# Layer 1's lists, expert weights and gate/up products, and layer 0's row gathers, in a two-layer mixture-of-experts kernel

## The reference

```
x = x + tanh(g_xattn[0]) * L0_xattn(layernorm(x), ctx, ...)   # router picks 2 of 64 context rows a token
x = x + tanh(g_ffn[0])   * L0_ffn(layernorm(x), ...)          # 32 experts, 6 a token, at most 192 tokens an expert
x = x + tanh(g_xattn[1]) * L1_xattn(layernorm(x), ctx, ctx)   # 16 heads, causal mask, 64 context rows
x = x + tanh(g_ffn[1])   * L1_ffn(layernorm(x), ...)          # 8 experts, 2 a token, and a shared expert

# an expert of L1_ffn: inner size I = 352
out = silu(x @ gw) * (x @ uw) @ dw
acc = acc + combine_weight[:, None] * out
```

## Time and profile before

| | |
|---|---|
| timed runs | 1188.62, 1192.48, 1199.31 us; median 1192.48 |
| the profiled execution | 1201.21 us, its span 1199.4 us |
| stage 1, until about | 235 us |
| stage 2 | 235 to 570 us |
| stage 3, and the wait for weights behind it | 570 to 868 us |
| stage 4 | 868 to 1199 us |
| busy share over the span | PE 89%, DVE 40%, POOL 32%, ACT 28% |

### The profile page before, as it was taken

The page is one execution under the profiler, slowest core; times in us unless marked ns, Lnnn a source line. Parts: engine busy times, 40 slices in busy tenths (PEclk is TensorE's granted clock), DMA queues, the critical chain, the costliest instruction groups (busy, mean ns, idle before and its releaser), DMA issues.

```text
span 1199.4 us, 13046 instructions
## 1 busy us (share of the span) xinstructions
PE 1063.8 (89%) x4351; PEld 707.0 (59%) x4351; DVE 480.3 (40%) x1148; ACT 331.4 (28%) x529; POOL 384.2 (32%) x340
## 2 busy tenths in 40 slices
PE   5777969579979999999599999899799999999995
PEld 4333424168769888886276766656355566556553
DVE  5767687224324444432684756451111111111110
ACT  3444441023323443332223423211012221222221
POOL 0003767625444555553002002220023233233322
PEclk9867979879989999999899999999899999999998
DMA  9110111379989989984503104219822332333330
GB/s 329 77 53 23 32 36 45 97 266 258 249 267 277 248 240 249 245 198 59 194 18 41 66 9 45 36 37 293 364 37 55 71 62 51 66 68 57 58 71 8
DMA packets 52801, 148.52 MB, mean 124 GB/s; under 512 B 12244, under 2 KB 12628, under 8 KB 47297
## 3 DMA queue, kind: packets, MB, share of 16 engines
q1 hardware_dynamic: 24752, 81.09, 21.4%
q0 software_dynamic: 24160, 44.03, 19.2%
q10 hardware_dynamic: 3824, 22.57, 5.5%
HBM read 109.76 MB, written 41.08 MB: 126 GB/s over the span
## 4 chain that ended last, share of the span: by engine, by line
PE 64%; DMA 15%; DVE 8%; issue 4%; POOL 4%; ACT 3%; SPq 0%; ACTq 0%; POOLq 0%; DVEq 0%
PE pb L586 16%; PE pb L602 8%; DMA acc_rows<-big 7%; PE pb L456 6%; PE pb L559 6%; PE pb L315 5%; PE pb L317 5%; PE pb L316 5%; DMA big<-hn_rows,big 4%; PE pb L322 4%; PE pb L378 3%; DVE big L908 2%; POOL list_rows L1300 2%; DVE big L916 2%; POOL acc_rows L1331 2%
## 5 line engine op out<-in xcount | busy, mean ns | idle before, releaser
L586 PE MATMUL pb<-big 128*128 x624 | 193.7, 464 | 5.5 <-issue 5.5
L456 PE MATMUL pb<-big 128*128 128x192 f32 x1024 | 174.9, 330 | 2.1 <-ACT bigr L746 1.3
L456 PEld LDWEIGHTS pb<-big 128*128 128x128 f32 x1024 | 170.9, 193 | 6.1 <-issue 2.8
L586 PEld LDWEIGHTS pb<-big 128*128 128x128 f32 x624 | 116.7, 192 | 65.0 <-issue 8.0
L1331 POOL DMA_INDIRECT acc_rows<-big x64 | 95.9, 1498 | 138.8 <-DMA acc_rows<-big 47.8
L1300 POOL DMA_INDIRECT list_rows<-big x96 | 93.9, 978 | 139.0 <-DVE big L920 110.4
L315 PE MATMUL pb<-bigr 128*128 128x512 f32 (+2 forms) x320 | 132.2, 413 | 4.4 <-DVE bigr L908 3.5
L1358 POOL DMA_INDIRECT out<-big x39 | 61.8, 1585 | 207.3 <-ACT big L888 207.3
L316 PE MATMUL pb<-bigr 128*128 128x512 f32 (+2 forms) x320 | 127.5, 399 | 0.0
L317 PE MATMUL pb<-bigr 128*128 128x512 f32 (+2 forms) x320 | 127.3, 398 | 0.0
L916 DVE SCALAR_TENSOR_TENSOR big<-pb,big 128x512 f32<-128x512 f32 (+1 forms) x80 | 58.8, 735 | 143.4 <-PE pb L559 41.4
(11 more groups left out here) (124 smaller groups left out, 1160.7 us busy)
## 6 DMA issues: line engine op xcount, KB each, us to landing
big<-in_we SPq DMA_DIRECT2D x32, 1024.0 KB, 7.9
rawr<-in_we SPq DMA_DIRECT2D x32, 512.0 KB, 4.3
big<-in_we ACTq DMA_DIRECT2D x1, 8704.0 KB, 37.0
hn_rows<-big SPq DMA_DIRECT2D x32, 256.0 KB, 2.0
big<-in_we ACTq DMA_DIRECT2D x1, 6528.0 KB, 34.1
big<-in_x SPq DMA_DIRECT2D x4, 1024.0 KB, 15.4
acc_rows<-big SPq DMA_DIRECT2D x16, 256.0 KB, 4.7
big<-acc_rows SPq DMA_DIRECT2D x16, 256.0 KB, 4.3
```

Of the source, the lines that this page charges most:

```text
L456: r = e.matmul(ps[:, m * CAP:(m + 1) * CAP], WR[b % 4][:, at_:at_ + 128], XT[b % 2][:, k, :], start=(k == 0), stop=(k == 3))
L586: r = e.matmul(ps[:, 0:I1], XT1[b % 2][:, k, :], W1[:, bass.ds(r0 + (q * 4 + k) * I1, I1)], start=(k == 0), stop=(k == 3))
```

## The change

1. **Layer 1's lists on TensorE.** `scatter1`, `lists1` and `turnl1` go. For each half block, DVE builds one-hot matrices of the list slots (`hote`, `hotv`, 128x512 each), POOL multiplies one of them by the token number and by the rounded weight (`hot`, two 128x512 products), PE multiplies them (`hotm`, four fp32r matmuls of 384 columns), DVE sums (`lsum`, 128x384). At the end come `lsumw`, `lturn`, `lcopy`, `lsel` and `ids1`.
2. **Experts loaded one by one.** `w1a` and `w1b` on ACT's queue become eight steps `w1.0` to `w1.7` on SP's queue, each with a semaphore of its own; `w1.0` waits for `hotm.3.1`, `w1.4` for the last shared gate product. Tile b below 8 waits only for expert b. The copies of tiles 0 and 1 also wait until all of `put3` have landed (`l_o`), since their memory is reused.
3. **Three rounded gate and up products.** `upt` becomes `gatet` and `upt`, each 12 fp32r matmuls of 352 columns. For each tile ACT rounds the expert's gate and up weights (`wgh`, `wuh`: 128x1408 each) and DVE takes the rest (`wgl`, `wul`), and the transposed rows are split in the same way (`turnt` on ACT and now on DVE). Register reads of ETK stand on ACT, DVE and PE.
4. **Layer 0's rows three experts ahead.** Six buffers G in place of four; `fetch.n+3` stands where `fetch.n+2` stood; `fetch.2` also waits for the stores of `acc_rows`.
5. The tables `PE_1`, `ACT_1`, `DVE_1` and all of stage 3's are in a new order.

Its core:

```diff
+                    three(e, PB[2 + 2 * (b % 2) + q][:, 0:I1], [(XH1[b % 2][:, k, :], XL1[b % 2][:, k, :], wh[:, k * I1:(k + 1) * I1], wl[:, k * I1:(k + 1) * I1])
+                                                               for k in range(4)]).then_inc(s_pe, c.up())
...
+                elif kind in ("wgh", "wuh"):
+
+                    q, user = dict(wgh=(0, "gatet"), wuh=(1, "upt"))[kind]
+                    if b < E1:
+                        e.wait_ge(l_w1[b], 16)
+                    if b < 2:
+                        e.wait_ge(s_dve, dve_end3)
+                        e.wait_ge(s_pe, pe_end3)
+                        e.wait_ge(l_o[0], 128)
+                        e.wait_ge(l_o[1], 128)
+                    else:
+                        e.wait_ge(s_pe, pe(user, b - 2))
+                    if q == 0:
+                        regs[b] = e.value_load(ETK[0:1, b:b + 1], min_val=0, max_val=7 * WE1)
+                    prev()
+                    e.activation(WSP[b % 2][q][0], w1[:, bass.ds(regs[b] + 4 * I1 * q, 4 * I1)], ACT.Copy).then_inc(s_act, c.up())
...
+                    tensor(lo, w1[:, bass.ds(regs[b] + 4 * I1 * q, 4 * I1)], hi.bitcast(F32), ALU.subtract)
...
+                elif kind == "w1":
+
+                    if b == 0:
+                        e.wait_ge(s_pe, pe("routet1", 3))
+                        e.wait_ge(s_pe, pe("flip3", 3, 3))
+                        e.wait_ge(s_pe, pe("hotm", 3, 1))
...
+                    e.dma_start(S(b * WE1, WE1, mem=w1), a["we1"][b]).then_inc(l_w1[b], 16)
...
-        pool2 = words(lambda n: (f"fetch.{n + 2} " if n + 2 < E0 else "") + (f"add.{n - 1}" if n else ""), E0) + f" add.{E0 - 1}"
+        pool2 = "fetch.2 " + words(lambda n: (f"fetch.{n + 3} " if n + 3 < E0 else "") + (f"add.{n - 1}" if n else ""), E0) + f" add.{E0 - 1}"
```

More of the change, by code:

```diff
@@ L47, in constants @@
     c[:, C_INV:C_INV + 128] = 1.0 / 64
-    c[:, C_TK1:C_TK1 + 16] = p[:, None] + 128 * np.array(TILES)
+    c[:, C_TK1:C_TK1 + 16] = p[:, None] + 128 * np.array(TILES) + 1
+    c[:, C_TP] = 2049 + p
     l0 = np.zeros((TRASH0, 2), np.float32)
     l0[:, 0] = 2048 + np.arange(TRASH0) % CAP
[L51 to L57, removed]
@@ L59 @@
[L59 removed]
+    return c, l0
@@ L118, in program @@
         rawr = second_name("rawr", 17152, 34816, F32)
+        hots = second_name("hots", 1536, 3600, F32R)
+        BACK = REST_ + NCONST + 4 * D + 4 + 4 + 64 + 64
+        later = second_name("later", BACK, 53120, F32R)
+        slots = second_name("slots", BACK, BACK + 32 * I1, F32R)
+        inner = second_name("inner", BACK + 32 * I1 + 2048, 53120, F32)
+        with nc.sbuf_tensor("w1", [128, REST_], F32) as w1:
+            pass
         big = ctx.enter_context(nc.sbuf_tensor("big", [128, 53120], F32))
@@ L212, in program @@
         YS = [two(D, p1=HALF) for _ in range(4)]
+        G[4], G[5] = two(D, p1=HALF), two(D, p1=HALF)
         LB = ring(HALF, 2, p1=64)
@@ L572, in _ @@
                     else:
[L573 removed]
+                        e.wait_ge(s_dve, dv("turnt", b - 1))
                     flip(e, G1[b % 2], PB[0]).then_inc(s_pe, c.up())
[L575 to L580 removed]
+                elif kind in ("gatet", "upt"):
+                    q = 0 if kind == "gatet" else 1
+                    wh, wl = WSP[b % 2][q]
+                    e.wait_ge(s_dve, dv("turnt", b))
+                    e.wait_ge(s_dve, dv("wgl" if q == 0 else "wul", b))
                     if b >= 2:
                         e.wait_ge(s_dve, dv("mult", b - 2))
[L583 to L587 removed]
+                    three(e, PB[2 + 2 * (b % 2) + q][:, 0:I1], [(XH1[b % 2][:, k, :], XL1[b % 2][:, k, :], wh[:, k * I1:(k + 1) * I1], wl[:, k * I1:(k + 1) * I1])
+                                                               for k in range(4)]).then_inc(s_pe, c.up())
                 elif kind == "flipt":
@@ L893, in _ @@
             c = Counter()
+            regs = {}
             def prev():
@@ L1274, in _ @@
                     both(AC1[j % 2], PB[j][:, :], TG[:, 3:4], xr[b][:, j, :], ALU.mult, ALU.add)
+                elif kind == "turnt":
+                    e.wait_ge(s_act, av("turnt", b))
+                    if b >= 2:
+                        e.wait_ge(s_pe, pe("upt", b - 2))
+                    tensor(XL1[b % 2].rearrange("p a b -> p (a b)"), PB[0][:, :], XH1[b % 2].rearrange("p a b -> p (a b)").bitcast(F32), ALU.subtract)
+                elif kind in ("wgl", "wul"):
+                    q, user = dict(wgl=(0, "gatet"), wul=(1, "upt"))[kind]
+                    hi, lo = WSP[b % 2][q]
+                    e.wait_ge(s_act, av(kind[0:2] + "h", b))
+                    if b < E1:
+                        e.wait_ge(l_w1[b], 16)
+                    if b >= 2:
+                        e.wait_ge(s_pe, pe(user, b - 2))
+                    if q == 0:
+                        regs[b] = e.value_load(ETK[0:1, b:b + 1], min_val=0, max_val=7 * WE1)
+                    tensor(lo, w1[:, bass.ds(regs[b] + 4 * I1 * q, 4 * I1)], hi.bitcast(F32), ALU.subtract)
                 elif kind == "mult":
```

284 lines of the change are left out of this document (174 added, 110 removed).

## The result

The changed kernel is slower: 1227.86 us median of four runs (1218.82 to 1237.64) against 1191.99, a ratio of 1.028 (1.021 to 1.035). In a second measurement (e14) it was 1.031 (1.024 to 1.037). I had predicted 1192.0 and no change, with 1214.0 as the upper end of the range.

A forecast was written before the change was run, and what follows sets the result against it. Bounds: POOL's list writes ending stage 1, a chain of adds in stage 2, PE in stages 3 and 4, the weight load between. Terms +4 − 5 + 5.5 + 1 + 14 + 2 − 22 = −0.5 gave 1192.0 us, range 1172 to 1214.

The forecast's parts named there:

- Stage 2: Layer 0's experts: gathering rows three ahead gains only for the first six experts, −5 us (−12 to 0).
- the chain of adds stays: Stage 2: POOL's adds in HBM stay 9.53 us apart, though PE's 22.4 us of waits could go.
- my rivals: Stores not held, 1179.5 (0.12); stage 4 at PE's pace, 1179 (0.13); longer circle, 1214 (0.15); late lists, 1204 (0.10).
- the upper bound of 0: Stage 2: the slow end of the range −12 to 0 us for gathering rows three experts ahead.
- The transition: Between stages 3 and 4: stores land behind loads, first `gatet` 52.6 us after `w1.0`'s issue, +14 us (+9 to +19).
- rival one: Between stages 3 and 4: stores are not held behind loads, 12.5 us less, 1179.5 us; chance 0.12.
- Stage 4: Gate and up in fp32r: a circle through the engines gives 7.51 us a tile against 8.08, saving 22 us.
- The lists: Stage 3: `hotm` adds 5.5 us on PE, the other list and order terms net +1 (−4 to +10).
- the 1.8 that hide them: Stage 3: POOL's products stay hidden while each takes less than 1.8 us; +2 us put on them.
- the 1 us that I had named as a sign: Stage 3: the changed profile should show `hotm` without waits of over 1 us.
- Stage 1: End of stage 1: the new order ends `place.3` some 11 us later, 6.7 hidden, +4 us (0 to +8).
- The sum: Whole kernel: all terms together come to −0.5 us, 1192.0 us predicted; chance 0.50.

The follow-up runs named there:

- e14: The changed kernel unedited, measured again beside other runs on one chip: 1238.31 us, 1.031 of the kernel before.
- e3: The kernel before with only layer 0's rows gathered three experts ahead (six buffers): 1224.62 us, 1.019 of before.
- e1: The changed kernel with layer 0's rows gathered two experts ahead again (four buffers, old POOL order): 1210.43 us, 1.010 of before.
- e2: The changed kernel with `split` ahead of `yout` on ACT and DVE in stage 2: 1209.72 us, 1.004 of before.
- e10: The changed kernel with the 1 MB load ahead of the 0.5 MB load on SP's queue in stage 2: 1213.75 us, 1.017 of before.
- e11: The changed kernel with six output buffers in place of four in stage 2: 1206.91 us, 1.010 of before.
- e4: The changed kernel with the last stores between the weight loads on SP's queue: 1211.25 us, 1.007 of before.
- e7: The changed kernel with loads `w1.0` to `w1.7` on ACT's queue and the stores alone on SP's: 1218.7 us, 1.024 of before.
- e13: The changed kernel with `split` ahead of `yout`, `turnt` ahead of `wuh`, and the expert loads on ACT's queue: 1181.06 us, 0.985 of before.

## Why the prediction was wrong

**Stage 2 is the step that failed.** I wrote that with rows three experts ahead PE's waits could go, "but the chain of adds stays", and put −5 on it with 0 as the upper bound. Three things were wrong in that. PE's waits for rows did not go: they are 28.6 us in stage 2, 22.4 before. The chain of adds has no pace of its own: the adds are 6.7 to 7.5 us apart at the end of stage 2, behind the last weight load (landed at 550.7), and 7.0 to 13.7 ahead of that, by what is under way beside them. And I did not ask what PE, when it runs further ahead of the adds, reaches next: the output buffers, two experts deep, with `yout` at the head of DVE's queue. Before, `yout` hardly had to wait (4.6 us for adds in all of stage 2 on DVE, against 119.3 after). The change added that wait on DVE, where `split` and behind it 1.5 MB of loads stand in line. This is the question that I had put to SP's queue at the transition, and did not put to DVE's in stage 2. None of my rivals had it; the upper bound of 0 had no reason behind it that excluded a loss. That the cause is this line of waits is shown by e3, which adds the fetch alone to the kernel before, and by e1, e2, e10 and e11, which each take away another link of it: with all links the adds take 310.7 to 312.6 in six traces and 318.3 in a seventh, with one of them missing 273.5 to 295.8 in eleven.

**The transition** was right in kind: stores behind loads in one queue, shown by e4, and rival one, shown by e7 to hold only for two queues. The size was 57.7 in place of 52.6 from issue to first gate product. `put3.3.0` landed 48.6 behind `w1.0`'s issue where I had 45.3, and the two stores and copies took 9.1 in place of 7.3. In rival one I had misread a row and left out a price: 861.46 is `out3.3.3`, not `out3.3.2`, and for a landing beside loads I had 3, where three of before's own last stores took 10.3, 12.9 and 12.4 us. With such landings the first `gatet` comes after 44 us, as in e7, and not after 40.

**Stage 4** was right to 0.13 us a tile: 7.64 against 7.51, the term that was short being the gaps at ACT (0.18 ahead of `wuh`) and PE's 0.20 behind DVE. Copies took 1.38 and 1.63, against 1.40 and 1.63. Passes of 352 columns followed at 0.16. Over 39 tiles the 0.13 are 5 us. The first two tiles took 9.5 and 9.2, some 3 more together than two of the rest, for which I had 2: PE had waited for 25 us ahead of tile 0, its granted clock fell from 1.00 to 0.50 (the lower of its two levels, 1.2 GHz) in that wait, and the first passes, up to 923.6, follow at 0.29. By the Trainium skill, TensorE: Matmul & The Clock Gate, The mechanism (Part 3), a weight load overlaps matmuls in flight only where its row group differs, so the 24 loads should have stood between the passes; the trace disagrees here too, for 24 passes from 999.75 take 3.9 us with a load in each. The same section names loads into a background weight buffer as a second case; which buffer these loads went to no run shows.

**The lists** cost 8.9 for 6.5 (7.7 as the mean of all traces with the lists, against the two without). POOL's products took 1.24 on average, under the 1.8 that hide them, one of the sixteen 1.94, and `hotm` waited for DVE's `hotv` for 2.4 in all, about the 2 that I had put on POOL; one of these waits was 1.40, over the 1 us that I had named as a sign. PE's long wait at the front of the stage is 12.4 in place of 8.8, where I had 3 more, and the wait of 4.08 is gone, as I had it. The rest, `hote`, `hotv` and `lsum` on DVE, I had not costed as waits of others, and no run tells it apart.

**Stage 1**: a wait of POOL of 5.03 where I had 4. Its effect on the time was not shown by the undo, and over all traces the first add comes 1.6 later with the new tables, so most of the +6.4 in the table is scatter between executions; that it came near my +4 is luck.

**The sum** came to −0.5 and the trace to +36.4: 22 of the 37 are stage 2, 5 the transition, 5 stage 4, 5 stages 1 and 3 together. In this pair of traces all of them erred to the same side, the optimistic one. Without stage 2 the time would by this sum have been some 15 over the prediction, near 1207 and inside the range, so what put it outside is that one step. The runs that undo it alone agree: e1, e2, e10 and e11 took 1.004 to 1.017 of before.

## What to carry to other kernels

When a prefetch goes deeper, name the next thing that the freed engine will wait for, and read what stands behind that wait in the queue in which it stands: here a load issue behind it made all transfers leave at once. Small transfers that others wait for belong ahead of bulk loads on a queue, not behind them, and putting them on another queue gets only a part of that (13 of the 22 us here). On a circle through several engines, move ahead of the bulk work that one step which the next engine waits for.

## What the runs showed of the hardware

Beside weight loads that kept the DMA engines full (426 GB/s in e7, 429 in e13), each of the four 256 KB stores on another queue took 10.3 to 11.5 us in place of 2.0. On the loads' own queue they landed behind all the loads issued ahead of them (`w1.7` at 909.87, `put3.3.0` at 910.5). The time of stage 2 scattered much more where it was not in lock step (273.5 and 289.4 for the same program) than in it (310.7 to 312.6 in six traces, 318.3 in one); what decides between the patterns within an unlocked stage stays open. POOL's elementwise products of 128x512 took 1.03 to 1.94 us, 1.24 on average, where DVE's subtraction of that shape took 0.69. In five of the eight halves POOL's second product ran beside the products of `hotv` on DVE, of the same shape, and both were longer: POOL's took 1.48 to 1.50, in the other three halves 1.03 or 1.04, and the longer of DVE's 1.34 to 1.56, without POOL beside it 0.69.
